# Four transformer layers, one sequence at a time: the layers behind the first run in turn over different sequences, and PSUM is given out in single banks

## What is computed

```
x = x + L0_attn_a(layernorm(x))   # "band": 16 heads of 64, RoPE, window of 128 keys back
x = x + L0_ffn(layernorm(x))      # "ffn0": silu(x Wg) * (x Wu), then Wd, hidden 384
x = x + L0_attn_b(layernorm(x))   # "causal": 16 heads of 8, RoPE
x = x + L0_ffn(layernorm(x))
x = x + L1_attn_a(layernorm(x))   # "chunk": 16 heads of 8, inside chunks of 64 tokens
x = x + L1_ffn(layernorm(x))      # "ffn1": tokens, hidden values and weights rounded to FP4 in blocks of 16
x = x + L1_attn_b(layernorm(x))   # "lowrank": 16 heads of 8, rank 32
x = x + L1_ffn(layernorm(x))
```

## Time and profile before

| | |
|---|---|
| median of 3 runs | 2160.3 us (2159.53 to 2160.73) |
| profiled execution | 2163.2 us, span of its instructions 2161.4 us |
| TensorE busy | 83% of the span, mean granted clock 0.94 |
| VectorE, GpSimd, ScalarE busy | 62%, 45%, 37% |

### The profile page before, as it was taken

The page is one execution under the profiler, slowest core; times in us unless marked ns, Lnnn a source line. Parts: engine busy times, 40 slices in busy tenths (PEclk is TensorE's granted clock), DMA queues, the critical chain, the costliest instruction groups (busy, mean ns, idle before and its releaser), DMA issues.

```text
span 2161.4 us, 51722 instructions
## 1 busy us (share of the span) xinstructions
PE 1786.3 (83%) x21261; PEld 1250.1 (58%) x21261; DVE 1348.4 (62%) x2749; ACT 801.5 (37%) x1298; POOL 978.4 (45%) x1362
## 2 busy tenths in 40 slices
PE   2899999999999998878999997777776778888883
PEld 2566666666666666655555555666666455555553
DVE  5744445555545543574555655677776788888873
ACT  0233333333333332324444444233343444444441
POOL 1523222333332222453333335589987555555543
PEclk9999999999999999989999999889988888888886
DMA  4000000000000000023323332233433122222200
GB/s 160 1 2 1 1 1 2 1 1 1 1 1 1 1 1 1 16 48 75 70 74 74 74 74 60 55 75 82 90 80 70 46 61 64 64 65 65 64 21 8
DMA packets 167465, 89.54 MB, mean 41 GB/s; under 512 B 9393, under 2 KB 165810, under 8 KB 166978
## 3 DMA queue, kind: packets, MB, share of 16 engines
q1 hardware_dynamic: 167010, 85.70, 16.7%
q0 software_dynamic: 224, 0.54, 0.1%
HBM read 46.36 MB, written 39.85 MB: 40 GB/s over the span
## 4 chain that ended last, share of the span: by engine, by line
PE 51%; DVE 27%; ACT 8%; issue 6%; POOL 6%; DVEq 0%; DMA 0%; POOLq 0%; ACTq 0%; SPq 0%
PE slots L1309 36%; DVE nmx L1201 11%; PE ctx_ps L1309 10%; DVE rope_part L1242 6%; ACT probs L1087 3%; DVE rope_part L1166 2%; PE slots L1584 2%; ACT ctxT L1007 1%; DVE ctxT L1285 1%; DVE rope_part L1167 1%; ACT band_va L1007 1%; ACT band_va L1023 1%; POOL band_rb L632 1%; POOL band_rb L631 1%; PE slots L1373 1%
## 5 line engine op out<-in xcount | busy, mean ns | idle before, releaser
L1201 DVE TENSOR_REDUCE nmx<-slots 128x8 f32<-128x1024 f32 (+2 forms) x352 | 408.1, 1217 | 115.0 <-PE slots L1309 113.6
L1087 ACT ACTIVATE probs<-slots 128x1024 f32<-128x1024 f32 (+1 forms) x416 | 355.7, 892 | 306.8 <-PE slots L1309 303.6
L1309 PE MATMUL slots<-band_r 64*64 64x64 bf16 (+4 forms) x5120 | 389.2, 261 | 82.4 <-DVE nmx L1201 42.0
L1309 PEld LDWEIGHTS slots<-band_r 64*128 64x128 bf16 (+2 forms) x5120 | 192.7, 120 | 252.5 <-issue 127.9
L1242 DVE SCALAR_TENSOR_TENSOR rope_part<-slots,bias_qk,rope_band 128x256 f32<-128x256 f32 x512 | 212.4, 477 | 196.9 <-PE slots L1309 173.1
L1309 PE MATMUL ctx_ps<-probs,band_va 64*32 64x64 f32 (+4 forms) x5120 | 261.2, 313 | 45.7 <-issue 22.1
L986 POOL TENSOR_TENSOR band_r<-rope_part 128x512 f32<-128x512 f32 x128 | 164.4, 1284 | 250.7 <-DVE rope_part L1242 250.7
L1309 PE MATMUL slots<-mask,ident_bf 128*128 128x256 bf16 (+1 forms) x896 | 217.9, 325 | 45.3 <-DVE nmx L1201 16.2
L1309 PEld LDWEIGHTS ctx_ps<-probs,band_va 128*32 128x32 f32 (+2 forms) x5120 | 145.2, 117 | 129.1 <-issue 66.4
L1309 PE MATMUL slots<-nmT,pick 64*128 64x256 bf16 (+2 forms) x2560 | 217.1, 240 | 0.9 <-issue 0.9
L900 POOL TENSOR_TENSOR var_eps<-mean_var,eps 128x2 f32<-128x2 f32 x128 | 29.2, 228 | 410.4 <-DVE mean_var L1129 410.4
(11 more groups left out here) (173 smaller groups left out, 2899.2 us busy)
## 6 DMA issues: line engine op xcount, KB each, us to landing
band_r<-scratch SPq DMA_DIRECT2D x192, 192.0 KB, 4.2
scratch<-parts SPq DMA_DIRECT2D x96, 192.0 KB, 2.2
scratch<-parts SPq DMA_DIRECT2D x96, 128.0 KB, 2.1
scratch<-parts SPq DMA_DIRECT2D x96, 64.0 KB, 1.8
x<-in_x SPq DMA_DIRECT2D x16, 128.0 KB, 2.7
out<-x SPq DMA_DIRECT2D x16, 128.0 KB, 1.8
band_r<-in_band_qk_a SPq DMA_DIRECT2D x1, 1024.0 KB, 6.3
band_r<-in_band_qk_b SPq DMA_DIRECT2D x1, 1024.0 KB, 7.9
```

Of the source, the lines that this page charges most:

```text
L1087: nc.scalar.activation(probs[:, g % 2, step[2], :, 0:width], slot(u, step).rearrange("p (a n) -> p a n", a=2)[:, :, 0:width], ACT.Exp, sca ...
L1201: nc.vector.tensor_reduce(dst, src, axis=AX.X, op=ALU.max, negate=True).then_inc(free_sem(u, step), 1)
L1309: return nc.tensor.matmul(o, lhsT, rhs, start=start, stop=stop, skip_group_check=shared)
```

## The change

First, the list of units. All bands still come first. Behind them one round holds one unit of each other kind, of different sequences: causal of sequence *i*, chunk of *i*-3, lowrank of *i*-6, end of *i*-9. Every wait that named "the unit before" now names the unit before of the right sort (`ATT_PREV`, `SMALL_PREV`, `PLAIN_PREV`, `QUANT_PREV`), and the two buffers for the operands of the small attentions go by a count of small units (`ring_at`) instead of by the sequence's number.

Second, PSUM. The six banks are given out singly: a fill that writes at most 512 columns (`narrow`) takes one bank; `score`, `S`, `scale`, band's `qk` and `v`, `qk` of causal and chunk, and the larger feed-forward fills take a pair. Six semaphores for single banks stand beside the three for pairs, and `take` waits for each fill that held one of the banks, so up to two waits. The `qk` of lowrank writes its two results side by side in one bank.

Third, new numbers in `LEAD`, from which `make_plan` draws a new order for every engine, in the band stage too. No instruction of computation is added or removed, and none changes its shape.

```diff
-UNITS = [(kind, b) for kind in (*ATTENTIONS, "end") for b in range(BATCH)]
+LAG = 3
+UNITS = [("band", b) for b in range(BATCH)]
+UNITS += [(kind, i - LAG * k) for i in range(BATCH + 3 * LAG) for k, kind in enumerate((*SMALL, "end")) if 0 <= i - LAG * k < BATCH]
+BANKS = 2 * SLOTS
+def narrow(kind, step):
+    name = step[0]
+    if name == "v":
+        return kind != "band"
+    if name == "qk":
+        return kind == "lowrank"
+    if name == "ffn":
+        return step[1] == 2 and AHEAD[kind] == "ffn0"
+    return name in ("xT", "down", "nm", "den", "rden", "ctx", "ctxT", "out")
...
-        "maxima": {"band": 15.183, "causal": -0.256, "chunk": 0.135, "lowrank": -1.548},
+        "maxima": {"band": 0.004, "causal": 0.799, "chunk": -0.003, "lowrank": 1.09},
...
-            slots[u, step] = slot, len(held[slot])
-            held[slot].append(released_by(u, step))
+            if narrow(UNITS[u][0], step):
+                free_now = [i for i in range(BANKS) if at[i] < UNKNOWN and at[i] + WAKE["pe"] <= start]
+                first = max(free_now, key=lambda i: (at[i ^ 1], -i))
+                taken, sem = [first], SLOTS + first
+            else:
+                first = min(range(0, BANKS, 2), key=lambda i: (max(at[i], at[i + 1]), i))
+                taken, sem = [first, first + 1], first // 2
+            waits = {held[i]: None for i in taken if held[i] is not None}
+            slots[u, step] = first, sem, counts[sem], tuple((slots[fill][1], slots[fill][2] + 1) for fill in waits)
...
-                        pe.wait_ge(slot_free[at], filled)
-                    return slots[:, at, :]
+                    for i, filled in SLOT[u, step][3]:
+                        pe.wait_ge(slot_free[i], filled)
+                    return slot(u, step)
```

More of the change, by code:

```diff
@@ L288 @@
     "pe": {
[L289 to L292, removed]
-        "maxima": {"band": 15.183, "causal": -0.256, "chunk": 0.135, "lowrank": -1.548},
-        "back": {"band": -2.437, "causal": -0.43, "chunk": -0.634, "lowrank": -1.541},
+        "tail": {"band": 0.101, "causal": 0.495, "chunk": 0.179, "lowrank": 0.18},
@@ L295 @@
+        "finish": {"causal": 0.409, "chunk": 15.782, "lowrank": -0.189, "end": -0.237},
+        "forward": {"causal": -0.143, "chunk": 7.606, "lowrank": -0.001, "end": 0.502},
+        "operands": {"band": 0.082, "causal": 7.848, "chunk": 0.115, "lowrank": -0.204},
+        "maxima": {"band": 0.004, "causal": 0.799, "chunk": -0.003, "lowrank": 1.09},
+        "back": {"band": -0.081, "causal": 0.119, "chunk": -0.062, "lowrank": -0.248},
     },
     "act": {
-        "tail": {"band": 53.895, "causal": 17.872, "chunk": 17.73, "lowrank": 16.182},
@@ L298 @@
[L298 to L301, removed]
+        "tail": {"band": -28.625, "causal": -0.924, "chunk": -89.046, "lowrank": 15.825},
+        "finish": {"lowrank": -0.766, "end": -9.759},
+        "forward": {"causal": -0.609, "chunk": 22.563, "lowrank": -0.959, "end": 2.226},
@@ L302 @@
+        "operands": {"band": -8.938, "causal": 0.194, "chunk": -0.542, "lowrank": -1.057},
+        "back": {"band": 1.528, "causal": -0.872, "chunk": -0.274, "lowrank": -0.5},
     },
     "dve": {
[L304 to L307 removed]
@@ L308 @@
-        "maxima": {"band": 32.94, "causal": 14.633, "chunk": 16.275, "lowrank": 22.45},
+        "tail": {"band": 6.2, "causal": -4.793, "chunk": -21.112, "lowrank": 0.777},
+        "finish": {"causal": -11.015, "chunk": -3.567, "lowrank": -4.933, "end": -11.061},
+        "forward": {"causal": 24.26, "chunk": 33.529, "lowrank": -3.199, "end": 2.152},
+        "operands": {"band": 6.858, "causal": 52.511, "chunk": -3.796, "lowrank": 5.797},
+        "maxima": {"band": 5.014, "causal": -19.073, "chunk": 12.131, "lowrank": 3.828},
@@ L400, in make_plan @@
                 if eng == "pe" and step[0] in FRONT_FILLS + BACK_FILLS:
-                    if slot is None or any(w not in done for w in opens[u, step]):
+                    slot_at = narrow_at if narrow(UNITS[u][0], step) else wide_at
+                    if slot_at == UNKNOWN or any(w not in done for w in opens[u, step]):
                         continue
```

173 lines of the change are left out of this document (101 added, 72 removed).

## The result

The kernel after takes 2171.4 us, the median of 10 runs (2166.0 to 2175.8), beside 2160.8 us of the kernel before in 10 runs (2156.0 to 2165.3). The ratio is 1.0047, with a 95% interval of 1.0036 to 1.0058: 0.5% slower, where I forecast 0.9% faster.

A forecast was written before the change was run, and what follows sets the result against it. TensorE was taken to bound band and causal, GpSimd chunk's core, TensorE and VectorE alternating in lowrank. Band's 24 us gain and the mix's 4 us loss took 2160.3 to 2140 us, own range 2125 to 2156, 8 in 10 2108 to 2175.

The forecast's parts named there:

- Part 1, band: Band stage: the new order and single banks save 1.5 us per unit, 24 us for 16 units.
- seven named waits: TensorE's short waits where one band unit's tail meets the next unit's scores: 2.02 us a unit, 0.5 expected to stay.
- the lower bound: Band: gain of nothing, if the removed waits only reappear at the eight `qk` fills.
- Part 2, the mixed rounds: Causal, chunk, lowrank and end units interleaved, 970 to 2050 us: same TensorE work, about even, taken as 4 us slower.
- the lowrank stretch: Lowrank with end, 1730 to 2050 us before the change: its 19.8% TensorE idle was taken for the mix, giving 1083 us.
- the 0.38 us ahead of `den`: Band: a narrow fill's wait for a slot held by a score, expected to go since one bank of a pair suffices.
- The clock falls in the causal work: Rival, mixed rounds: causal's 330 us get the lowrank clock of 0.88, costing 31 us; median 2171; chance 0.22.
- The mix is filled: Rival, mixed rounds: kinds cover each other's waits, idle falls to 17%, mix 34 us shorter, median 2102; chance 0.20.
- The change does nothing in band: Rival, band: `scale` and `qk` take back what other waits gave; 2164 us or no change; chance 0.08.
- a stop of 1.5 to 2.7 us per chunk `V`: Sign, mixed rounds: TensorE still stops once in each chunk unit's `V`, about 24 us for 16.
- clock under 0.88 over the rounds: Sign, mixed rounds: a clock this low would show that the rival of a falling clock is right.

The follow-up runs named there:

- e7: Kernel after, with every engine's order up to the end of the band layer taken from the kernel before, banks single: 2161.6 us.
- e8: Kernel before with single banks, with order and banks up to the end of the band layer taken from the kernel after: 2158.1 us.
- e6: Kernel after with each lowrank score matmul and each matmul of band's `scale` fills issued twice: 2150.5 us.
- e9: Kernel after with only the matmuls of band's `scale` fills issued twice, lowrank scores once: 2160.5 us.
- e1: Kernel after with two 128x512 matmuls added per band unit ahead of the `rden` transposes, into a bank overwritten anyway: 2165.1 us.
- e4: Kernel before, order unchanged on every engine, with PSUM banks given out singly to narrow fills: 2142.9 us.
- e2: Kernel after with each lowrank score matmul issued twice, the second overwriting the first with the same values: 2160.6 us.
- e11: e4 with two of the eight row-maximum reductions of every lowrank unit made twice on VectorE: 2181.8 us.
- e10: e7 with two of the eight row-maximum reductions of every lowrank unit made twice on VectorE: 2204.2 us.

## Why the prediction was wrong

**Part 1, band: the step that failed.** I priced seven named waits of 2.02 us a unit, 1.5 of them as gone, and took 24 us for 16 units. The twelve units of the landmark got 7.0 us longer instead; by e7 and e8, all with single banks, the new band order costs 10 to 15 us. Two things went wrong with it.

- *The waits were only moved.* The ones that I named did go, but 2.13 us of others stand at the join. Over a whole unit the idle time fell from 38.6/12 = 3.2 us to 33.4/12 = 2.8 us: 0.4 us, a quarter of my 1.5. I had put the reappearing at the `qk` fills as the lower bound; it came at `rden`, the scores, `xT` and `scale`. VectorE's `ctxT` steps pace the four `scale` fills one by one, and in the new order nothing stands between them.
- *The clock.* `scale` now comes last ahead of `out`, but for one score fill, thin and with waits, and the clock falls during `out`. TensorE's busy time per unit went up from 569.0/12 = 47.4 us to 581.2/12 = 48.4 us, 1.0 us, which is more than the waits gave. That it is the clock, and that it hangs on the `scale` stretch, is shown by e6 and e9, which give 10 to 11 us back with added matmuls, and by the units of after itself, 51.7 us with a fall and 50.1 to 50.5 without. That the doubled `scale` fills stop the falls and the two matmuls at `rden` don't is measured (e1), not understood.

Even with the clock whole (e9) a unit takes 50.3 us: 0.3 us a unit less than before, 5 us in all, and not 24. Most of that is the single banks, since before's order has 50.4 with them; e9 and e7, 2160.5 and 2161.6 us, are level.

**Part 2, the mixed rounds: right as a net, and by offset.** Behind the 13th band unit the kernel after takes 7.6 us more than before, where I had 4, and e7, whose clock is whole in band, takes 2158.7 - 766.2 = 1392.5 us, level with before's 1392.8. The idle share that I borrowed from the lowrank stretch, 19.8%, is 19.7% over the rounds. But the net hides two terms that I hadn't told apart: single banks give 12.1 us there (e4), and the mixed order takes 11.9 of them back by the profiled spans, 13 to 19 us by the medians. Between e7 and after stand another 1400.4 - 1392.5 = 7.9 us. The last three band units are in them: the 16th row of the landmark starts at 888.3 us in e7 and at 896.8 in after, 8.5 later, where the 13th was 3.7 later, so 4.8 us are band's. Behind it, where the orders are the same, stand 3.1 us, with the clock at 0.91 and 0.89 over 970 to 2050 us.

**The banks, a gain that I didn't price by itself.** I credited them only with the 0.38 us ahead of `den`. Alone they are worth 17.4 us, most of it behind the 13th band unit. I had not asked what each half of the change would do without the other.

**The rivals.** *The clock falls in the causal work* gave 2171 us, and 2171.4 was measured. It was right in its mechanism and its sign, and half right in its place: the clock over 970 to 1300 us is 0.92 instead of 1.00, but about as much was lost in band, which I had taken as safe at 1.00 (10.9 us come back there by e9, and 10.8 in the rounds by e2, of which before's order gives 5.9 as well). e6, with both doublings, prices what could be bought back at 2171.4 - 2150.5 = 21 us. That the number fits is luck: it is 31 us of slower causal work on top of a band gain of 24 that didn't come, and TensorE's busy time rose by 14.2 us in all. The page of the Trainium skill that I named for it ("TensorE: Matmul & The Clock Gate", section "A second HAM failure mode: psum-queue depth-cycling") describes short idles between groups of matmuls as enough to make the clock swing. The trace agrees: the single idles ahead of the fall in band are 0.58 us and less. What I drew from it for the single banks did not come: alone (e4) they leave the mean clock at 0.940, as before. *The mix is filled* fell by its idle share. *The change does nothing in band* was nearly right on the waits, and did not have the clock.

**Of what was to show it:** the waits ahead of `den` and for `nmT` gone, yes; waits ahead of `scale` stay, yes, and grew; a unit 1.5 us shorter, no; TensorE near 20% idle and `DVE nmx` its largest releaser, yes; GpSimd under 70% in a long stretch, yes; a stop of 1.5 to 2.7 us per chunk `V`, nearly, 13 stops of 22.6/13 = 1.7 us in the mean between 970 and 2050 us, the longest 3.8; clock under 0.88 over the rounds, no, 0.89. The bound for that last sign was set for falls in the rounds alone; half of what filling bought back stood ahead of them.

## What to carry to other kernels

A wait that is named and removed is not a gain until one has asked which resource sets the pace of the stretch, since the wait forms again at the next fill that depends on it. Before a reordering, look at what will stand thin, in short matmuls with short waits, right ahead of a long step: in band the clock's fall was paid mostly in the long step and not in the thin one, and a few repeated matmuls in the right gaps can be cheaper than none. And take a change with two mechanisms apart first: here single banks alone were 0.9% faster than before, and the order made for them took more than that away.

## What the runs showed of the hardware

- 512 added matmuls made the same kernel 10.8 us faster (e2), and 128 added in the band's `scale` fills 10.9 us (e9). Two matmuls a unit half a dozen steps earlier (e1) left the falls in `out` where they were, though TensorE idled as little: 30.3 us in twelve units, and 30.8 in e9.
- Neither the longest single idle nor the idle share told whether the clock would fall. It fell in after, where no idle in the twelve band units is longer than 0.58 us and they sum to 33.4 us. Over the same units it stayed whole in before, with 38.6 us, and in e4, with 38.1 us and an idle of 0.79 us ahead of the first `S` of every unit.
- In after, a band unit with a fall of the clock takes 51.7 us, and one without 50.1 to 50.5.
- 39 us of VectorE time ahead of the release of a bank cost 39.0 us in the old order, 36.3 of them TensorE's idle time (e11), and 42.6 us in the mixed one, 18.5 idle and 25.2 slower matmuls by the profiled spans (e10).
